# Core bias as two 64-row products, first two relation pairs by node groups, clearing and self bias on GpSimd

## The chip, the cores and the metric

The kernel runs on one core of one Trainium2 chip. The metric is the device time of one execution in microseconds. A measurement is the median of several executions.

## The reference

Two graph layers over 3125 nodes with 256 features, 100,000 edges sorted by destination, 64 edge features and 16 edge types. What is computed, cut to the core:

```
h  = relu(layernorm(x))
ei = concat(h[src], edge_attr)                       # 256 + 64 per edge
core = relu(ei @ W1 + b1) @ W2 + b2
gate = sigmoid(ei @ Wg + bg)
agg  = segment_sum(gate * core, dst)
x    = x + layernorm(agg + h) * gamma + beta
h  = relu(layernorm(x))
forward:  sum over edges into dst of (h @ Wf[type])[src] + forward_bias,  divided by the in-degree
backward: sum over edges into src of (h @ Wb[type])[dst] + backward_bias, divided by the out-degree
x    = x + 2 * h @ loop_weight + self_bias + forward + backward
```

## The kernel before

Nodes lie in 25 blocks of 128, edges in 196 supertiles of 512 (four tiles of 128). Every matrix product of the dense parts is split into three products of rounded high and low parts (PARTS). Each engine runs its own instruction list in order; semaphores tie them together, and there is no planner: the order is written out by hand. It runs in these stages.

*Tables* (to 78 us): layer norm of x, and a table ptab of h @ W1 and h @ Wg for every node, stored in memory.

*Message stage* (to about 1454 us): one pass for each supertile s. GpSimd gathers 4 x 128 rows of ptab into pbuf (two buffers, so the gather for s starts when the first sums of s-2 are done). TensorE runs `edge_products(s)`: twelve 64-row products for the gate into pg (L643), twelve for the hidden layer into pu (L651), both in pairs that lie on the two halves of the array (HALVES: edge features of two tiles are stacked in 64 + 64 partitions), then a wait for the gather and eight transposes of the gathered rows added into pu (L657). Then `core(s-1)`: a wait for s_ulo (low part of the hidden layer), a wait for s_msg (VectorE has read pc), and for each of the two banks of pc a bias product (L666: 128 rows by 512 columns; ones_k times bias_k, of which only the first two partitions are not zero: high and low part of b2) and twelve products with W2 (L671). Then `sum_messages(s-2)`, a one-hot product that sums edges by node (L680), and for supertiles that reach into a further node block a second one. VectorE for each supertile: low part of the edge features (L976), gate sum (L971), low part of the hidden layer (L980), message = gate x core out of pc (L1000), one-hot (L994), addition to acc (L1078), low part of the message (L1006). ScalarE makes the high parts, the relu and the sigmoid.

*Node stage* (to about 1530 us): five groups of five node blocks (GB = 5). VectorE for group g: statistics of acc (L836), scales for the second norm of the group before (`ln_scales`, L844 and L845), centre, residual, low part of the transposed blocks (`evacuate_hT`, L857), statistics of res. ScalarE: `node_group(g)`: square roots, the normalised blocks (L438), high parts of the transposed blocks (L526), and copies of projected blocks to pstage (`evacuate`, L261). TensorE: transposes of five blocks (L602), then `project(0, ...)` for them, six products of 512 columns each block (L775). A projection covers a pair of relations q. Five banks (pslots) and five pstage buffers are used in turn, block b uses b % 5; SyncE stores pstage to proj. `slot b` may be written when the copy before it is done (s_pev) and copied when the store before it has landed (s_pst).

*Forward projections* (to 1775 us): TensorE projects all 25 blocks for q = 1, then q = 2 to 7. ScalarE casts the weights' high part (`weights_high`, L541), VectorE makes the low part (`weights_low`, L1156), then sorts: 12 steps of max and match-replace (L1210, L1213) for each q on the edge keys. Ahead of the sort VectorE clears acc (L1199) and adds the self bias to res (L1200); behind it, it writes the rows for the gathers of proj, which start then, and adds the own products (`own` on TensorE, L620; `add_own`, L861).

*Second layer's sums* (to the end): forward gathers and one-hot sums, with the backward projections between them, then backward gathers and sums.

## Time and profile before

| | us |
|---|---|
| runs before | 3843.88, 3847.81, 3848.78 (median 3847.81) |
| profiled execution | 3849.95 |
| its span, first to last instruction | 3848.1 |

| Engine | busy us | share of the span | instructions |
|---|---|---|---|
| TensorE products | 3288.7 | 85% | 21136 |
| TensorE weight loads | 2831.0 | 74% | 21137 |
| VectorE | 2579.7 | 67% | 3930 |
| GpSimd | 2340.2 | 61% | 2362 |
| ScalarE | 976.2 | 25% | 1654 |

The span in 40 equal slices of 96 us; each digit is the busy share in tenths (9 is 90% or more), PEclk the granted clock of TensorE in tenths of full speed:

```profile
PE   6999999999999996998777778878857778787776
...
DVE  6888888888888887887766673333354444444444
ACT  3555555555555544442000000000010000000000
POOL 1666655666665660002776677777777777777775
PEclk8999999999999998999989899999989999999999
```

Slices 2 to 15 are the message stage, slice 16 holds the node stage, slices 17 to 19 the forward projections. In the profile PE is TensorE, PEld its weight loads, DVE VectorE, ACT ScalarE, POOL GpSimd, SP SyncE; L12 is line 12 of the kernel before. Durations of matrix products are modelled ends and overlap, so what a product costs in a full stream is read from the distance of starts or from the chain of work.

### The profile page before, as it was taken

The numbers are of one execution on the slowest core, as the hardware profiler recorded it, in microseconds if no ns is written. First come the engines' busy times: TensorE is split into PE (matmuls) and PEld (weight loads), VectorE is DVE, ScalarE is ACT, GpSimd is POOL, SyncE is SP. The second block draws the span as 40 slices with busy tenths as digits, with TensorE's granted clock in tenths as the row PEclk, the third lists the DMA queues.
The fourth block names the chain that finished last, engine by engine and source line by source line (L and its number), as shares of the span: only waits on it lengthen the run. The fifth ranks groups of instructions, "written<-read, shape, count | busy, mean of one in ns | idle before, by whom it ended". The sixth has DMA issues, their size and how long they took to land.

```text
span 3848.1 us, 74572 instructions
## 1 busy us (share of the span) xinstructions
PE 3288.7 (85%) x21136; PEld 2831.0 (74%) x21137; DVE 2579.7 (67%) x3930; ACT 976.2 (25%) x1654; POOL 2340.2 (61%) x2362
## 2 busy tenths in 40 slices
PE   6999999999999996998777778878857778787776
PEld 4999999999999995887665566666645666665654
DVE  6888888888888887887766673333354444444444
ACT  3555555555555544442000000000010000000000
POOL 1666655666665660002776677777777777777775
PEclk8999999999999998999989899999989999999999
DMA  5666666666565652664555557555533333333333
GB/s 173 174 171 171 172 171 168 171 168 169 167 169 164 170 160 84 208 209 160 158 163 153 151 154 164 166 157 161 160 97 105 104 102 98 100 105 104 104 105 114
DMA packets 322741, 569.88 MB, mean 148 GB/s; under 512 B 73895, under 2 KB 218389, under 8 KB 322581
## 3 DMA queue, kind: packets, MB, share of 16 engines
q0 software_dynamic: 137984, 411.19, 38.5%
q1 hardware_dynamic: 182732, 154.33, 12.2%
q10 hardware_dynamic: 1864, 2.52, 0.2%
q8 instruction: 65, 1.06, 0.1%
q14 instruction: 96, 0.78, 0.1%
HBM read 452.43 MB, written 115.41 MB: 148 GB/s over the span
## 4 chain that ended last, share of the span: by engine, by line
PE 64%; DVE 15%; issue 10%; POOL 4%; DMA 3%; DVEq 2%; ACT 1%; SPq 1%; ACTq 0%; POOLq 0%
PE pc L671 14%; PE pa L680 13%; PE pa L719 7%; PE pu L657 5%; DVE tops L1210 5%; PE pu L719 4%; PE pg L643 4%; DVE key L1213 4%; PE pg L719 4%; POOL fa L422 4%; PE pu L651 3%; PE pc L666 2%; DMA fa<-proj,gslot 2%; PE pu L775 2%; PE pg L775 1%
## 5 line engine op out<-in xcount | busy, mean ns | idle before, releaser
L422 POOL DMA_INDIRECT fa<-proj,gslot x1568 | 1503.5, 959 | 882.0 <-issue 436.8
L405 POOL DMA_INDIRECT fa<-ptab,slot x784 | 832.9, 1062 | 576.5 <-issue 298.9
L680 PE MATMUL pa<-fa,onehot 128*128 128x258 f32 x1760 | 471.0, 416 | 212.3 <-DVE onehot L994 141.4
L671 PEld LDWEIGHTS pc<-ws,hr 128*128 128x128 f32 x4704 | 607.1, 188 | 16.8
L671 PE MATMUL pc<-ws,hr 128*128 128x256 f32 x4704 | 614.0, 279 | 0.0
L994 DVE SCALAR_TENSOR_TENSOR fa<-pc,base,src_f 128x512 f32<-128x512 f32 x406 | 303.6, 751 | 450.0 <-PE pa L719 320.0
L680 PEld LDWEIGHTS pa<-fa,onehot 128*128 128x128 f32 x1760 | 349.6, 205 | 319.2 <-issue 264.0
L719 PE MATMUL pa<-fa 128*128 128x258 f32 x1568 | 373.5, 380 | 0.0
L719 PEld LDWEIGHTS pa<-fa 128*128 128x128 f32 x1568 | 297.0, 189 | 45.2
L719 PE MATMUL pu<-fa 128*128 128x258 f32 x784 | 198.9, 397 | 120.7 <-DVE acc L1051 82.5
L1000 DVE TENSOR_TENSOR fa<-fa,pc 128x1024 f32<-128x1024 f32 x196 | 239.4, 1221 | 92.4 <-PE pc L671 92.3
L495 ACT CAST hr<-fa 128x1024 fp32r<-128x1024 f32 x196 | 206.4, 1053 | 362.3 <-DVE fa L1000 362.3
L719 PEld LDWEIGHTS pu<-fa 128*128 128x128 f32 x784 | 146.5, 194 | 170.2 <-DVE acc L1051 112.8
L719 PE MATMUL pg<-fa 128*128 128x258 f32 x784 | 194.4, 390 | 85.9 <-issue 85.2
L484 ACT ACTIVATE hr<-pu 128x512 fp32r<-128x512 f32 x392 | 213.3, 596 | 189.1 <-PE pu L657 189.1
L580 ACT COPY gslot<-row_dst 128x8 int32 (+1 forms) x98 | 19.3, 197 | 953.6 <-DMA fa<-proj,gslot 953.6
L1026 DVE TENSOR_TENSOR acc<-acc,pa 128x258 f32 x196 | 82.7, 422 | 261.1 <-PE pa L680 258.7
L1006 DVE TENSOR_TENSOR hr<-fa,hr 128x1024 fp32r<-128x1024 f32 x196 | 240.1, 1225 | 24.8 <-ACT hr L495 9.1
L680 PE MATMUL pa<-hr 128*128 128x256 f32 x1760 | 247.5, 283 | 5.8 <-issue 3.7
L775 PE MATMUL pu<-hr 128*128 128x512 f32 x960 | 251.6, 406 | 0.0
L719 PEld LDWEIGHTS pg<-fa 128*128 128x128 f32 x784 | 145.0, 192 | 132.4 <-issue 112.2
L489 ACT ACTIVATE fa<-fa 128x1024 f32<-128x1024 f32 x196 | 208.1, 1062 | 130.7 <-DVE fa L971 130.7
(151 smaller groups left out, 4934.9 us busy)
## 6 DMA issues: line engine op xcount, KB each, us to landing
proj<-fa SPq DMA_DIRECT2D x400, 256.0 KB, 2.3
fa<-in_ea_t SPq DMA_DIRECT2D x196, 128.0 KB
fa<-proj,gslot POOLq DMA_INDIRECT x1568, 2.8
fa<-ptab,slot POOLq DMA_INDIRECT x784
fa<-in_Wrel SPq DMA_DIRECT2D x32, 256.0 KB, 3.0
ptab<-fa SPq DMA_DIRECT2D x25, 256.0 KB, 2.0
out<-res SPq DMA_DIRECT2D x4, 768.0 KB
res<-in_x SPq DMA_DIRECT2D x1, 1792.0 KB, 20.4
```

What stands on the lines that cost most here:

```text
L405: pool.indirect_dma_start(pbuf[:, n % 2, j, :], None, ptab[:, :], bass.IndirectOffsetOnAxis(ap=slot[:, n, j:j + 1], axis=0)).then_inc(s_ga ...
L422: pool.indirect_dma_start(gbuf[:, n, j, 0:H], None, proj[k - 1][:, :], bass.IndirectOffsetOnAxis(ap=gslot[:, at, j:j + 1], axis=0)).then_i ...
L484: last = nc.scalar.activation(uT[:, par, 0, h, :, :].rearrange("p k e -> p (k e)"), pu[:, h, :], ACT.Relu)
L489: nc.scalar.activation(gate[:, par, :, :], gate[:, par, :, :], ACT.Sigmoid).then_inc(s_gate, 1)
L495: nc.scalar.copy(msg[:, par, 0, :, :], gate[:, par, :, :]).then_inc(s_mhi, 1)
L671: last = nc.tensor.matmul(pc[:, j, :], uT[:, par, a, j // 2, kk, j % 2 * P:(j % 2 + 1) * P], w2s[:, c, kk, :], start=False, stop=(j == jj ...
L680: last = nc.tensor.matmul(pa[:, bank, 0:width], keys[:, at, j, :], rows[:, j, :], start=(n == 0), stop=(n == len(todo) - 1))
L719: last = nc.tensor.matmul(out[:, 0:AW], onehot2[at // GS][:, at % GS, j, :], gbuf[:, n, j, :], start=(j == 0), stop=(j == J - 1))
L775: last = nc.tensor.matmul(pslots[n], hT[:, a, kk, b * P:(b + 1) * P], wsp[:, u, c, kk, :], start=(not d and m == 0 and kk == 0), stop=(m = ...
L994: return nc.vector.scalar_tensor_tensor(out=(onehot0, onehot, onehot2[at // GS])[k][:, at % GS, :, :], in0=nodes, scalar=base[:, bass.ds(b ...
L1000: nc.vector.tensor_tensor(gate[:, par, :, :], gate[:, par, :, :], pc[:, :, :], ALU.mult).then_inc(s_msg, 1)
L1006: nc.vector.tensor_tensor(msg[:, par, 1, :, :], gate[:, par, :, :], msg[:, par, 0, :, :], ALU.subtract).then_inc(s_mlo, 1)
```

## The change

Core bias: `core_bias(s)` writes each bank of pc with one 64-row product of 512 columns; the two banks' products lie on the two halves of the array (partitions 0 to 63 and 64 to 127 of ones_k and bias_k). For that b2 is also brought to partitions 64 and 65 (one more small DMA on ScalarE's queue, four more small VectorE operations). It is issued in edge_products(s) for supertile s-1, between the pu products and the gathered rows' transposes, with the wait for s_msg ahead of it; core() has neither any more. For the first and the last supertile it stands by itself.

First two relation pairs: within each node group TensorE projects the group for q = 0 and then for q = 1, with the next group's transposes in between (three ahead of q = 1's blocks, two among them). The order of the bank uses, of the copies on ScalarE and of the stores follows (slot_use, projected). weights_high(1) moves to ScalarE's first node group, weights_low(1) to VectorE's third loop turn ahead of the scales, weights_low(2) to behind the third step of the first sort.

GpSimd clears acc and adds the self bias, when all blocks are transposed; VectorE waits for that only ahead of add_own.

```diff
+        bias_raw2 = fa[DE:DE + 2, 6144:6144 + H].rearrange("p (d f) -> p d f", d=1)
+        def piped(q):
+            return isinstance(q, int) and q < 2
+        def slot_use(q, b):
+            return 2 * (b // GB) + q if piped(q) else 5 * q + b // 5
+        def projected(q, b):
+            return 2 * GB * (b // GB) + GB * q + b % GB if piped(q) else NB * q + b
         def evacuate(eng, copy, q, b):
-            n = b % 5
-            eng.wait_ge(s_proj, NB * q + b + 1)
-            if b >= 5:
-                eng.wait_ge(s_pst[n], 16 * (5 * q + b // 5))
-            elif past(q, 1):
-                eng.wait_ge(s_pst[n], 16 * 5 * q)
+            n, use = b % 5, slot_use(q, b)
+            eng.wait_ge(s_proj, projected(q, b) + 1)
+            if past(use, 1):
+                eng.wait_ge(s_pst[n], 16 * use)
...
# GpSimd, behind the gathers of the message stage
+            pool.wait_ge(s_hT[1], NB)
+            nc.gpsimd.memset(acc[:, :, :], 0.0).then_inc(s_zero[0], 1)
+            nc.gpsimd.tensor_tensor(res[:, :, :], res[:, :, :], sbias_b[:, :].unsqueeze(1).to_broadcast([P, NB, H]),
+                                    ALU.add).then_inc(s_sb, 1)
# ScalarE
             def weights_high(q, par, half):
-                    act.wait_ge(s_proj, NB * (q - 1))
+                    act.wait_ge(s_proj, 2 * NB - GB if isinstance(q, int) and q == 2 else NB * (q - 1))
                 if g == 0:
                     weights_high(0, 0, 0)
-                for n in range(GB + 1):
-                    if 1 <= g <= NB // GB and n < GB:
+                    weights_high(1, 1, 0)
+                for n in range(GB):
+                    if 1 <= g <= NB // GB:
                         normalise(2, group(g - 1)[n], res, ACT.Relu)
-                    if g >= 2 and n >= 1:
-                        evacuate(act, nc.scalar.copy, 0, group(g - 2)[n - 1])
-                    if 1 <= g <= NB // GB and n >= 1:
-                        transposed_high(group(g - 1)[n - 1])
+                    if g >= 3:
+                        evacuate(act, nc.scalar.copy, 1, group(g - 3)[n])
+                for n in range(GB):
+                    if 2 <= g <= NB // GB + 1:
+                        evacuate(act, nc.scalar.copy, 0, group(g - 2)[n])
+                    if 1 <= g <= NB // GB:
+                        transposed_high(group(g - 1)[n])
...
             weights_high(2, 0, 1)
-            for b in range(NB):
-                evacuate(act, nc.scalar.copy, 1, b)
+            node_group(NB // GB + 2)
# TensorE
+            def core_bias(s):
+                if past(s, 1):
+                    pe.wait_ge(s_msg, s)
+                for h, half in enumerate(HALVES):
+                    nc.tensor.matmul(pc[:, 2 * h:2 * h + 2, :], ones_k[half, :], bias_k[half, 0:1, :].to_broadcast([DE, 2, H]),
+                                     start=True, stop=False)
             def edge_products(s, par, pair):
...
+                if past(s, 2):
+                    core_bias(s - 1)
                 pe.wait_ge(s_gath[0][par], 16 * J * (pair + 1))
             def core(s, par):
                 pe.wait_ge(s_ulo, s + 1)
-                if past(s, 1):
-                    pe.wait_ge(s_msg, s)
                 for jj in range(0, J, 2):
-                    nc.tensor.matmul(pc[:, jj:jj + 2, :], ones_k[:, :], bias_k[:, 0:1, :].to_broadcast([P, 2, H]),
-                                     start=True, stop=False)
...
+            for b in group(0):
+                transposes(1, b)
             for g in range(NB // GB):
-                for b in group(g):
-                    transposes(1, b)
...
                     project(0, 0, b, 0)
-            pe.wait_ge(s_wlo, 2)
-            for b in range(NB):
-                project(1, 1, b, 0)
+                later = group(g + 1) if g + 1 < NB // GB else []
+                for b in later[:3]:
+                    transposes(1, b)
+                if g == 0:
+                    pe.wait_ge(s_wlo, 2)
+                for n, b in enumerate(group(g)):
+                    project(1, 1, b, 0)
+                    for t in later[3 + n:4 + n]:
+                        transposes(1, t)
# VectorE
             split_row(bias_k[0:2, :, :], bias_raw)
+            split_row(bias_k[DE:DE + 2, 0:1, :], bias_raw2, DE)
-                if g == 1:
-                    weights_low(0, 0)
+                if g in (1, 2):
+                    weights_low(g - 1, g - 1)
...
-            weights_low(1, 1)
             dve.wait_ge(s_hT[1], NB)
...
-            nc.vector.memset(acc[:, :, :], 0.0).then_inc(s_zero[0], 1)
-            nc.vector.tensor_tensor(res[:, :, :], res[:, :, :], sbias_b[:, :].unsqueeze(1).to_broadcast([P, NB, H]),
-                                    ALU.add).then_inc(s_sb, 1)
-            dve.wait_ge(s_zero[0], 1)
-            dve.wait_ge(s_sb, 1)
...
                 for n in range(S1):
                     sort_step(before + 2 * n, n)
+                    if also and n == 2:
+                        weights_low(2, 0)
```

## Rows read from the trace of the kernel before

**Rows 1.** Busy time by stretch: busy us (instructions) by engine, clock, DMA, GB/s.
```profile
400.00:1400.00 1000.00, 999.53 (x9610) 948.50 (x9608) 889.61 (x1044) 508.28 (x788) 607.51 (x573) 1.00 0.61 169
1461.00:1540.00 79.00, 52.64 (x219) 40.39 (x220) 63.24 (x200) 37.65 (x87) 0.00 (x0) 0.82 0.27 92
```

**Rows 2.** Chain that ended last, one supertile: start us, us, what.
```profile
1005.91 0.23 PE pc L666
1006.14 1.40 PE pc L671 x12
1007.54 0.23 PE pc L666
1007.77 1.41 PE pc L671 x12
1009.18 0.95 PE pa L680 x8
1010.13 0.90 PE pg L643 x12
1011.03 0.71 PE pu L651 x12
1011.74 1.02 PE pu L657 x8
```

**Rows 3.** Waits, 400 to 1400 us, VectorE: total us, times, longest.
```profile
DVE fa L1000 <- PE pc L671: 68.0, 143, 1.2
```

**Rows 4.** Timeline, a gather's last issue: start us, us, engine, line.
```profile
1005.83 1.01 POOL L405 DMA_INDIRECT fa<-ptab,slot  x1 [0.30 <-issue]
```

**Rows 5.** Chain that ended last, a gather's landing.
```profile
1248.14 3.53 DMA fa<-ptab,slot
```

**Rows 6.** Timeline, start of the message stage, [idle before, releaser].
```profile
80.20 0.55 DVE L900 CAST bias_k<-fa 2x512 fp32r<-2x512 f32 x1
...
82.08 0.74 DVE L903 SCALAR_TENSOR_TENSOR bias_k<-fa,ident,bias_k 2x512 fp32r<-2x512 f32 x1
...
88.22 1.55 PE L643 MATMUL pg<-ws,hr 64*128 64x256 f32 x12 [0.46 <-DVE fa L971]
```

**Rows 7.** Timeline, second node group.
```profile
1479.87 4.06 PE L775 MATMUL pu<-hr 128*128 128x512 f32 x12
...
1481.07 1.72 DVE L836 BATCH_NORM_STATS2 stats<-res 128x6 f32<-128x256 f32 x5
...
1485.48 0.17 DVE L845 SCALAR_TENSOR_TENSOR nmr<-mv,rstd 128x5 f32<-128x5 f32 x1
```

**Rows 8.** Chain that ended last, projections of the node stage.
```profile
1483.93 2.72 PE pg L775 x12
...
1492.13 4.34 PE pu L775 x12
```

**Rows 9.** Groups, ScalarE, 1461 to 1547 us: busy us, mean ns, idle before.
```profile
L438 ACT ACTIVATE acc<-res,nmr,rstd 128x256 f32<-128x256 f32 x25 | 14.7, 606 | 1.6 <-DVE nmr L845 1.6
L261 ACT COPY fa<-pu 128x512 f32<-128x512 f32 x13 | 7.4, 581 | 1.5 <-PE pu L775 1.5
```

**Rows 10.** Timeline, VectorE from the node groups into the sort.
```profile
1530.26 0.42 DVE L857 TENSOR_TENSOR hr<-pa,hr 128x256 fp32r<-128x256 f32 x1 [0.34 <-ACT hr L526]
...
1534.10 5.43 DVE L1199 MEMSET acc<- 128x6450 f32 x1 [1.41 <-issue]
...
1546.30 1.23 DVE L1156 TENSOR_TENSOR hr<-fa,hr 128x1024 fp32r<-128x1024 f32 x1
1547.44 0.97 DVE L1210 MAX8 tops<-key 128x8 f32<-128x784 f32 x1
...
1554.36 0.98 DVE L1210 MAX8 tops<-key 128x8 f32<-128x784 f32 x1
```

**Rows 11.** Timeline, end of the projections and of the sort.
```profile
1774.78 1.58 PEld L620 LDWEIGHTS pa<-ws,hr 128*128 128x128 f32 x12
...
1782.97 0.17 DVE L1219 COPY srt<-tops 128x16 f32<-128x16 f32 x1
```

More of the change, by code:

```diff
@@ L26 @@
 EPS = 1e-5
-NW = 11
+NW = 12
 XA = 10
@@ L345, in _ @@
             sp.dma_start(wlraw.rearrange("p (k f) -> p k f", k=HK), Wl.rearrange("(k p) f -> p k f", p=P)).then_inc(s_w2, 16)
-            with sp.Fori(0, NQ // 4) as i:
+            for q in range(2):
+                sp.wait_ge(s_wlo, q + 1)
+                load_weights(q + 2, q)
+            for g in range(NB // GB):
+                for q in range(2):
+                    store_projections(q, 0, group(g))
+            with sp.Fori(1, NQ // 4) as i:
                 relations(i, 0)
@@ L1247, in sort_region @@
                     keep_sorted(before + 2 * steps, SI // 2 * i + S2 * u, steps)
-            weights_low(2, 0)
-            for q in range(2):
-                sort_relation(q)
+            sort_relation(0, also=True)
+            sort_relation(1)
             with dve.Fori(1, NQ // 4) as i:
```

27 lines of the change are left out of this document (15 added, 12 removed).

## Prediction

> **What bounds the kernel now.** I read four views in this order. First the busy time by stretch [rows 1]: in the message stage (92 to 1454 us) TensorE is busy 999.5 of 1000 us at the full granted clock (1.00, the 2.4 GHz level), while VectorE has 110 us to spare; in the node stage behind it (1461 to 1540) TensorE is busy 52.6 of 79 us and its granted clock is 0.82 on average. So the same TensorE instruction is worth its full time in the first stretch and perhaps nothing in the second. Second, the chain of work that ended last, through one supertile of the message stage [rows 2]: eight TensorE pieces that sum to 6.85 us, nothing else between them. The two bias products are two of them, 0.23 us each. Third, VectorE's waits there [rows 3]: 68.0 us over 143 supertiles are waits for the core products, so 0.475 us of a supertile is what TensorE could give up before VectorE takes over. Fourth, the order of time from the end of the message stage to the second layer's gathers [rows 10, 11]: VectorE closes the node groups at 1530.68, clears sums and adds the self bias until 1546.3, starts sorting at 1547.44 and ends at 1783.1; TensorE has finished projecting before, at 1774.8. There VectorE's chain sets the end.
>
> **The core bias.** Removed are 2 x 196 products of 128 rows by 512 columns at 0.23 us each: 0.46 us a supertile, all on the path [rows 2]. Added are two products of 64 rows by 512 columns, one on each half of the array, behind the other 64-row products of edge_products. The trace of before has no 64-row product of 512 columns. Nearest rows: twelve 64-row products of 256 columns take 0.71 us, or 0.059 each, and twelve 128-row ones of the same width take 1.40, or 0.117 [rows 2]. So two halves run side by side in the time of one, and the pair should cost what one 512-column product costs, 0.23 us. Bounds: 0.12 (the pair as cheap as four 256-column pieces at half of 0.059) and 0.46 (one after the other). I take 0.23, as it follows from both rows. The group L657 already follows a 64-row group today, so no change of mode is added. Saved: 0.23 x 196 = 45 us, bounds 0 and 67.
>
> The wait for s_msg moves with it: the bias of supertile s-1 is issued in edge_products(s), so it waits for messages(s-2) 0.95 + 0.90 + 0.71 = 2.56 us after the core products of s-2 end [rows 2]. Behind it in TensorE's queue stand the gathered rows' transposes, and ScalarE and VectorE wait for those. That message product starts right at the end of the core products and takes 1.22 us, so 1.3 us are left: I cost the wait at nothing. It costs 0.1 us for every 0.1 us by which VectorE is later than that.
>
> What is late next: VectorE needs (1000 - 68) / 143 = 6.52 us a supertile against 1000 / 143 - 0.23 = 6.76 for TensorE, so 0.24 us stay [rows 1, 3]. The gathers are closer. Four are issued in a row; the last began at 1005.83, took 1.01 and needs 3.5 us to land, so 1010.4, and the transposes that read it come at 1011.74 [rows 2, 4, 5]. 1.4 us are left, and a gather has two supertiles, so 0.46 of it goes. Some gather instructions take longer than that one, so a few supertiles will wait. I take 4 us for it, with bounds 0 and 25 (0.13 us in each). Message stage: -45 + 4 = -41 us, likely -20 to -46.
>
> **The start.** The bias is split a second time on VectorE, four small operations in a chain. The first four took from 80.20 to 82.82, 2.6 us, for 512 columns; now 256. Behind them on VectorE stands the first gate sum, for which TensorE already waited 0.46 us, so all of it counts [rows 6]. With the added DMA issue ahead of ScalarE's first work: +2 us, bounds 0 and 3.5.
>
> **The node groups.** Here I have to build the new order. Let N(g) be the moment at which VectorE has the scales of group g's predecessor ready, 1485.65 for g = 2 [rows 7]. Prices: a projected block 1.36 (2.72 for two) [rows 8], its copy by ScalarE 0.58, a normalised block 0.6 [rows 9], two transposes 0.25 (a quarter of L657's 1.02) [rows 2], a low part 0.42 and weights_low 1.2 [rows 10], a high part as much as a low one (an estimate, it reads the same tile) and the cast of weights 1.1 likewise, statistics 2.12 a group and scales 0.35 (1481.07 to 1485.65 holds two and one) [rows 7].
> - weights_low(1) now stands ahead of the scales for g = 2: 1.2 us, N(2) = 1486.9. ScalarE normalises five blocks (to 1489.8) and copies one projected block, TensorE projects two blocks with two transposes between them until 1493.5; high and low part, two statistics and scales give N(3) = 1499.
> - From g = 3 on each normalised block is followed by the copy of relation 1's block of three groups back, and only that copy frees the bank for relation 0's next group. So TensorE waits for N(g) + 1.2, projects five blocks (6.8), transposes three (0.75), then block, transpose, block, transpose (3.2): N + 12.0. Latency and high and low part 1.0, two statistics 4.25, scales 0.35: 17.6 us a group, where today's products of two groups start at 1479.87 and 1492.13, 12.3 apart [rows 7, 8]. TensorE works 15 of these and still idles 2.6. N(4) = 1516.6; N(5) needs one statistic less but waits for a square root: 1532.4.
> - The last low part ends 13.0 later, at 1545.4, where it was 1530.7 [rows 10]: 14.7 us later.
> - Then clearing and adding, 12.2 us from 1534.10 to 1546.30, are gone from VectorE, and so are the two weights_low in front of the sort. Sorting starts at about 1546.5 against 1547.44 [rows 10].
>
> So the move to GpSimd only pays back what the new coupling takes. Then three steps run (6.92 us, to 1553.4) [rows 10], and VectorE waits for the high weights of relation 2, behind which the whole sort is queued. ScalarE has these after TensorE's last block of relation 0: N(5) + 16.1 + 6.8 = 1555.3, copy and cast 1.7, weights_low 1.2: 1558.3, where three steps were done at 1554.36 before. That is +3.9 us, and the sort behind it is unchanged. After sparse transposes TensorE fell to half clock today and took 4.34 us for twelve products that otherwise take 2.72 [rows 1, 8]; three groups can meet that, 0 to +4.8. I take +5 in all, bounds -6 (below) and +12.
>
> GpSimd's part is hidden: it needs to be done when VectorE adds the own products, after 1783, 236 us later [rows 10, 11]. Even at ten times VectorE's 12.2 us it is. If that cover were gone, it would be 12 us or more. TensorE's earlier end of relation 1 is worth nothing: relation 3 needs weights that VectorE makes between sorts, and the gathers wait for the sort's end too. From there on nothing changes.
> The Trainium skill speaks against this move: "GPSIMD Engine Reference", Engine selection, puts a two-input elementwise addition at about twice VectorE's time; by it the addition takes some 14 us (an estimate). It would add that only if it stood on the path; no run here shows it yet.
>
> **Sum.** Profiled execution 3849.95 us (span 3848.1 and 1.9 around it). 3849.95 - 41 + 2 + 5 = 3816. The median of the runs, 3847.81, lies 2.1 below that execution, so I forecast 3814.
>
> **The rivals.**
> - *Another resource takes over in the message stage.* For: gathers have 1.4 us of slack and VectorE 0.24 after the change; the gather queue shows instructions of uneven length. Against: TensorE waited for them almost never over 1000 us. If half of the 45 are lost: 3850 - 22 + 7 - 2 = 3833. Chance 0.15.
> - *The node groups gain.* If VectorE keeps its pace, the second products only fill TensorE's gaps: 45 blocks and their transposes from 1479.8 on, 61.2 + 5 us, end at 1546.0; copy, cast and low part 2.9: 1548.9, 5.5 us earlier than 1554.36. Then 3850 - 41 + 2 - 5.5 - 2 = 3803. Against it: the bank that is freed only behind N(g). Chance 0.15.
> - *The sort is slowed by GpSimd.* Both work in SBUF for 20 us or so; if VectorE's steps took half as long again in that time, 10 us more: 3824. Chance 0.05. "GPSIMD Engine Reference", Specifications, of the Trainium skill, says that the two engines get in each other's way where VectorE's instruction has two SBUF inputs or runs in a two-port mode; the sort's steps have one large input, and by that rule this does not happen.
> - *The two 64-row products do not run side by side* (slower). Both write pc, in two banks, with 512 columns each, a form no row shows. Then the pair costs 0.46, nothing is saved, and start and node groups remain: 3850 + 2 + 5 - 2 = 3855. If each also pays the 0.19 us by which L643 is above L651 for entering its mode, 3892. It decides from a pair of 0.42 us on. Against it: L651 does just this with 256 columns. Chance 0.08.
> - My forecast, 0.57.
>
> **How the numbers follow.** A measurement of this kernel tells about 0.2% from no change, 7.7 us: faster is below 3840, slower above 3855.5. The forecast's own range is 3804 to 3828 (message stage -32 to -46, node groups 0 to +10). The 8 in 10 take in the first two rivals: 3797 to 3838. Faster 0.86; same 0.06 (a gather-bound stage with a bad node stage, part of the fourth rival); slower 0.08.
>
> **What would show it.** In the profile after: a message-stage period of about 6.62 us with the pair at 0.23 in the chain; VectorE's wait for the core products near 0.24 a supertile; waits for ptab gathers in front of the transposes, few; node groups some 17.5 us apart, with the last low part near 1545 and a wait of VectorE for ScalarE's weights near 1554; the sort's end near 1749 (1788 less the 41 of before, plus 2 of the start). The forecast is wrong if the pair costs over 0.3 us, if the bias waits for VectorE, or if the node groups stay at 12 us.

## The result, and the profile after

The changed kernel takes 3816.88 us, the median of four executions (3810.56 to 3823.66); the kernel before, on the same chip, 3846.21 (3843.88 to 3848.78). The ratio is 0.9926, with a 95% interval of 0.9914 to 0.9938: faster by 0.6 to 0.9%. The forecast was 3814, with 3797 to 3838 as the range. The profiled execution took 3810.56 us, its span is 3808.5. One of the five executions of same_half (below) took 6646.73 us at a mean granted clock of 0.53, where its other four have 0.96, and is left out of that kernel's median.

The head of the page of after (busy us, share of the span, instructions of each engine):

```profile
span 3808.5 us, 74360 instructions
...
PE 3248.9 (85%) x21136; PEld 2785.6 (73%) x21137; DVE 2569.9 (67%) x3932; ACT 976.4 (26%) x1654; POOL 2352.2 (62%) x2364
```

The chain of work that ended last, after, one supertile of the message stage (start us, us, what), which answers to [rows 2]:

```profile
1003.46 0.95 PE pa L708 x8
1004.41 0.90 PE pg L673 x12
1005.31 0.71 PE pu L681 x12
1006.02 0.24 PE pc L661 x2
1006.25 1.03 PE pu L689 x8
1007.28 2.81 PE pc L699 x24
1010.09 0.95 PE pa L708 x8
```

The two bias products (L661) are one piece of 0.24 us behind the other 64-row products, where [rows 2] has two pieces of 0.23; the supertile takes 6.63 us instead of 6.85. It is still TensorE from end to end.

The waits of 400 to 1300 us, after (us in total, times, longest), which answer to [rows 3] and to the gathers of [rows 4, 5]:

```profile
DVE fa L1036 <- PE pc L699: 34.4, 76, 0.9
...
PEld pu L689 <- DMA fa<-ptab,slot: 1.5, 4, 0.4
```

The stretch holds 133 supertiles (900 us at 6.78 us each, the 1321.5 us from the first core product to the last by 195; some supertiles carry a further one-hot product, so the mean is above the 6.63 of a plain one). A supertile has 34.4 / 133 = 0.26 us left before VectorE would be late (0.475 in [rows 3]), and TensorE waited for a gather four times, 1.5 us in all.

The node groups of after: VectorE's scales (nmr) from the third on (the first are at 1435.00), and what TensorE waited for (start us, us, idle before and its releaser in brackets), against [rows 7, 8]:

```profile
1459.66 0.16 DVE L881 SCALAR_TENSOR_TENSOR nmr<-mv,rstd 128x5 f32<-128x5 f32 x1
1477.26 0.17 DVE L881 SCALAR_TENSOR_TENSOR nmr<-mv,rstd 128x5 f32<-128x5 f32 x1
1493.29 0.17 DVE L881 SCALAR_TENSOR_TENSOR nmr<-mv,rstd 128x5 f32<-128x5 f32 x1
...
1461.08 2.97 PE L805 MATMUL pu<-hr 128*128 128x512 f32 x12 [2.56 <-ACT fa L272]
...
1478.68 3.00 PE L805 MATMUL pu<-hr 128*128 128x512 f32 x12 [2.56 <-ACT fa L272]
```

From the third to the fourth scales it is 17.60 us, and before each of these groups TensorE idles 2.56 us for ScalarE's copy (fa L272), which stands behind a norm in ScalarE's queue.

Into the sort and out of it, after, against [rows 10, 11]:

```profile
1506.18 0.42 DVE L893 TENSOR_TENSOR hr<-pa,hr 128x256 fp32r<-128x256 f32 x1 [0.86 <-ACT hr L548]
...
1507.10 0.98 DVE L1240 MAX8 tops<-key 128x8 f32<-128x784 f32 x1
...
1518.20 1.23 DVE L1193 TENSOR_TENSOR hr<-fa,hr 128x1024 fp32r<-128x1024 f32 x1 [4.33 <-ACT hr L563]
1519.35 0.97 DVE L1240 MAX8 tops<-key 128x8 f32<-128x784 f32 x1
...
1519.06 14.35 POOL L427 TENSOR_TENSOR res<-res,sbias_b 128x6400 f32<-128x6400 f32 x1 [6.89 <-issue]
...
1742.88 1.58 PEld L643 LDWEIGHTS pa<-ws,hr 128*128 128x128 f32 x12
...
1749.30 0.17 DVE L1249 COPY srt<-tops 128x16 f32<-128x16 f32 x1
```

The sort starts right behind the last low part, stops after three steps for 4.33 us (ScalarE's high weights of relation 2), and goes on beside GpSimd's addition, which takes 14.35 us where VectorE took 6.76. TensorE, which has projected relation 1 early, stops later for the low part of relation 3's weights, which stands in VectorE's queue behind the second sort:

```profile
1568.49 1.22 DVE L1193 TENSOR_TENSOR hr<-fa,hr 128x1024 fp32r<-128x1024 f32 x1
...
1569.85 5.48 PE L805 MATMUL pu<-hr 128*128 128x512 f32 x12 [12.45 <-DVE hr L1193]
```

Where the 39.6 us between the two spans come from: the first core product starts 1.6 us later (94.06 against 92.5); from there to the first statistics of the node stage 1328.7 us pass instead of 1369.4 (-40.7); from there to the sort's end 326.7 instead of 321.2 (+5.5); behind the sort 2059.0 instead of 2065.0 (-5.9). Nothing shows the last to be of the change: in the ten profiled executions on the chips of usual speed, of both biases and both orders of the projections, that stretch took 2059 to 2072 us, and executions of one kernel lie up to 20 us apart.

### The profile page after: what moved, and what is told of

It is laid out like the page before. It is cut to its first block, busy times and chain, and to the rows that moved or that the text cites. A ratio compares the mean times of both kernels' runs of the same rounds, so it can differ in the third digit from the quotient of the medians.

```text
span 3808.5 us, 74360 instructions
## 1 busy us (share of the span) xinstructions
PE 3248.9 (85%) x21136; PEld 2785.6 (73%) x21137; DVE 2569.9 (67%) x3932; ACT 976.4 (26%) x1654; POOL 2352.2 (62%) x2364
## 4 chain that ended last, share of the span: by engine, by line
PE 68%; DVE 13%; issue 10%; POOL 4%; DMA 3%; DVEq 2%; ACT 1%; ACTq 0%; POOLq 0%; SPq 0%
PE pc L699 14%; PE pa L708 13%; PE pa L747 7%; PE pu L689 5%; PE pg L673 4%; PE pu L747 4%; POOL fa L443 4%; PE pu L805 4%; PE pg L747 4%; DVE tops L1240 3%; PE pu L681 3%; PE pg L805 3%; DVE key L1243 3%; DMA fa<-proj,gslot 2%; DVE onehot L1030 1%
## 5 line engine op out<-in xcount | busy, mean ns | idle before, releaser
L699 PE MATMUL pc<-ws,hr 128*128 128x256 f32 x4704 | 598.8, 283 | 0.0
L708 PEld LDWEIGHTS pa<-fa,onehot 128*128 128x128 f32 x1760 | 349.4, 205 | 316.1 <-issue 261.1
L699 PEld LDWEIGHTS pc<-ws,hr 128*128 128x128 f32 x4704 | 565.4, 189 | 0.6 <-issue 0.6
L747 PE MATMUL pu<-fa 128*128 128x258 f32 x784 | 199.3, 397 | 118.2 <-DVE acc L1087 73.4
L805 PE MATMUL pg<-hr 128*128 128x512 f32 x960 | 241.1, 393 | 0.0
```

The costliest lines, as they stand in the source:

```text
L699: last = nc.tensor.matmul(pc[:, j, :], uT[:, par, a, j // 2, kk, j % 2 * P:(j % 2 + 1) * P], w2s[:, c, kk, :], start=False, stop=(j == jj ...
L708: last = nc.tensor.matmul(pa[:, bank, 0:width], keys[:, at, j, :], rows[:, j, :], start=(n == 0), stop=(n == len(todo) - 1))
L747: last = nc.tensor.matmul(out[:, 0:AW], onehot2[at // GS][:, at % GS, j, :], gbuf[:, n, j, :], start=(j == 0), stop=(j == J - 1))
L805: last = nc.tensor.matmul(pslots[n], hT[:, a, kk, b * P:(b + 1) * P], wsp[:, u, c, kk, :], start=(not d and m == 0 and kk == 0), stop=(m = ...
```

## Experiments

Three sets of four kernels. The first and the third ran on chips on which the kernel before took 3846.8 and 3845.8 us. The second set ran on a chip on which every kernel, the one before too, took 4510 to 4583 us; there only the node stage is read, from the traces. Common to all comparisons of that stage is the table below: us from the first scales of the node stage, in the profiled execution. Three kernels stand in it twice (after and after_again; pool_gated and gated_again; early_gated and early_again): the end of the sort repeats to 0.3, 1.5 and 0.2 us, so less than 1.5 us between two kernels says nothing.

| kernel | last scales | sort starts | TensorE's projections end | sort ends |
|---|---|---|---|---|
| before | 46.5 | 73.3 | 300.8 | 309.0 |
| after | 58.3 | 72.1 | 308.1 | 314.5 |
| after_again | 58.3 | 72.1 | 308.5 | 314.8 |
| bias_only | 46.8 | 73.4 | 302.7 | 309.8 |
| nodes_pool_only | 61.3 | 75.1 | 310.0 | 316.6 |
| bias_pool | 47.1 | 83.0 | 313.4 | 319.8 |
| pool_gated | 46.7 | 69.4 | 301.9 | 308.3 |
| gated_again | 47.6 | 70.0 | 303.4 | 309.8 |
| pool_late | 47.0 | 58.9 | 301.5 | 307.8 |
| early_gated | 53.0 | 65.7 | 297.0 | 303.4 |
| early_again | 53.0 | 65.8 | 296.4 | 303.2 |
| no_pool | 59.9 | 87.3 | 318.6 | 325.0 |
| same_half | 58.3 | 72.0 | 308.4 | 314.7 |
| no_bias | 59.9 | 73.7 | 309.8 | 316.1 |

### The change taken apart

bias_only is the kernel before with the new core bias alone:

```diff
+            def core_bias(s):
+                if past(s, 1):
+                    pe.wait_ge(s_msg, s)
+                for h, half in enumerate(HALVES):
+                    nc.tensor.matmul(pc[:, 2 * h:2 * h + 2, :], ones_k[half, :], bias_k[half, 0:1, :].to_broadcast([DE, 2, H]),
+                                     start=True, stop=False)
```

> The core bias alone is changed: pairs of 64-row products, the second split of b2; node groups, clearing and self bias stand as in the kernel before. My theory (message stage 40.7 us shorter between the first core product and the node stage, start 2 us longer, everything behind it as before): 39 us under the kernel before, ratio 0.990. Rival (part of the gain is given back in the second layer whatever the node stage does, since the changed kernel's median lies only 28 us below): about 30 us, ratio 0.992. Rival (the pair costs twice a single product): no gain.

Measured: 3805.77 us, the median of six (3803.50 to 3821.57), against 3846.83; ratio 0.9893, 0.9876 to 0.9910. That is 41 us less by the medians (39 were expected), and 11 less than the whole change; how firm the 11 are is told at after_again.

nodes_pool_only is the change without the new bias: the first two relation pairs projected by node groups, and GpSimd's two steps.

> The node groups with both relation pairs and the move to GpSimd alone; the core bias as before. My theory (a cycle of 17.6 us a group over the copies of relation 1's blocks, then a wait for relation 2's weights): the sort ends 5.5 us later than before, the total is 5 us above the kernel before, ratio 1.0014. Rival (it gains, as it fills TensorE's gaps): the sort ends earlier and the total is 5 us below. Rival (its cost is larger than the stage itself, because the later stages are disturbed): 10 us or more above.

Measured: 3860.22 us, the median of ten; ratio 1.0028, 1.0018 to 1.0038. The other half of the change costs 11 to 13 us, where 5 were expected: the way was right, the size missed. In the table its sort ends 7.6 us later than before's, 2.1 later than in the whole change; the other 3 to 6 us are not seen up to that point. The 2.1 go with the clock: twice the first twelve products of a group ran slowly, at a mean granted clock of 0.66 and 0.63, so partly at the lower of the two levels (1.2 and 2.4 GHz), where the same twelve take 2.97 and 3.00 us in after, at 1.00. TensorE's wait ahead of them is the same in both (2.56 to 2.58 us), so these rows don't say what decides it:

```profile
1500.21 4.38 PE L796 MATMUL pu<-hr 128*128 128x512 f32 x12 [2.58 <-ACT fa L271]
...
1519.22 4.52 PE L796 MATMUL pu<-hr 128*128 128x512 f32 x12 [2.56 <-ACT fa L271]
```

after_again is the changed kernel once more beside these.

> The changed kernel itself, unchanged, beside the other three on one chip. My theory: the sum of the parts, 39 - 5.5 = 33.5 us under the kernel before, ratio 0.9913, within the first measurement's interval (0.9914 to 0.9938) or just beside it. Rival (parts don't add up): 28 us, and then bias_only plus nodes_pool_only differ from it by 5 us.

Measured: 3816.30 us, the median of six (3806.29 to 3819.08); ratio 0.9911, 0.9897 to 0.9925. The sum of the parts, 33.5 us under the kernel before, was expected; it is 30.5. After minus bias_only is 10.5 us by the medians of the same set, of which the sort's end explains 5.0 (314.8 against 309.8). The other half is not firm: bias_only's six executions fall into four of 3803.50 to 3806.74 and two of 3819.08 and 3821.57, and by the means (3810.1 and 3814.9) the difference is 4.8 us. The profiled execution of bias_only was one of the two long ones, and it is behind the sort that it is long (2071.5 us, where after has 2059.0).

bias_pool is bias_only with GpSimd's two steps:

```diff
+            pool.wait_ge(s_hT[1], NB)
+            nc.gpsimd.memset(acc[:, :, :], 0.0).then_inc(s_zero[0], 1)
+            nc.gpsimd.tensor_tensor(res[:, :, :], res[:, :, :], sbias_b[:, :].unsqueeze(1).to_broadcast([P, NB, H]),
+                                    ALU.add).then_inc(s_sb, 1)
...
-            nc.vector.memset(acc[:, :, :], 0.0).then_inc(s_zero[0], 1)
-            nc.vector.tensor_tensor(res[:, :, :], res[:, :, :], sbias_b[:, :].unsqueeze(1).to_broadcast([P, NB, H]),
-                                    ALU.add).then_inc(s_sb, 1)
```

> The core bias and the move of clearing and self bias to GpSimd; the node stage and the order of projections as before. My theory: VectorE starts its sort 13.6 us earlier, but from then on waits for relation weights that follow TensorE's projections (before, only some 2 us lay between them), so the sort ends 2 us earlier than with the core bias alone: 41 us under the kernel before. Rival (VectorE's chain alone decides): 39 + 13.6 = 52 us under it.

Measured: 3814.68 us (3802.42 to 3821.81), ratio 0.9902, 0.9884 to 0.9920. Both the theory and the rival miss the stage: the sort was to end 2 us earlier than in bias_only or more, and ends 10.0 later. VectorE lost 12.2 us of work, and yet the sort starts 9.6 us later, at 83.0. The timeline of bias_pool, VectorE and GpSimd, shows why:

```profile
1492.71 1.22 DVE L1180 TENSOR_TENSOR hr<-fa,hr 128x1024 fp32r<-128x1024 f32 x1 [0.45 <-ACT hr L557]
...
1505.34 14.66 DVE L1180 TENSOR_TENSOR hr<-fa,hr 128x1024 fp32r<-128x1024 f32 x1 [11.08 <-ACT hr L557]
1519.92 0.96 DVE L1228 MAX8 tops<-key 128x8 f32<-128x784 f32 x1
...
1504.81 14.10 POOL L421 TENSOR_TENSOR res<-res,sbias_b 128x6400 f32<-128x6400 f32 x1 [7.01 <-issue]
```

The same instruction takes 1.22 us at 1492.71 and 14.66 at 1505.34, half a microsecond behind the start of GpSimd's addition; it is done 1.09 us after that ends (1518.91). The next relation's low part is late with it, and TensorE waits 8.8 us for that.

### What holds VectorE for 14.66 us

pool_gated is bias_pool with one wait more, which puts the addition behind that low part:

```diff
             nc.gpsimd.memset(acc[:, :, :], 0.0).then_inc(s_zero[0], 1)
+            pool.wait_ge(s_wlo, 3)
             nc.gpsimd.tensor_tensor(res[:, :, :], res[:, :, :], sbias_b[:, :].unsqueeze(1).to_broadcast([P, NB, H]),
```

> The new bias and GpSimd's two steps with the old order of the projections, as in the run bias_pool, and one wait more: GpSimd starts its addition only when VectorE has written the low part of relation 2's weights. In the trace of bias_pool that low part took 14.66 us (1505.34 to 1520.00) beside GpSimd's addition (1504.81 to 1518.91), where it takes 1.23 us elsewhere. My theory: VectorE's operation with two operands in SBUF is held until GpSimd's addition is over. Then it takes 1.2 us here, the sort starts near 1506.6 instead of 1519.9, TensorE's wait of 8.8 us for a later low part goes, and the sort ends near 1743.5 instead of 1756.8: 13 us less than bias_pool in the trace, a time near 3802. Rival: the 14.66 us has another cause (it waited for ScalarE's part); then it stays and so does the time (3814.7). GpSimd's addition itself should then take 14.1 us or less beside the sort.

Measured, timeline of pool_gated:

```profile
1682.10 1.23 DVE L1181 TENSOR_TENSOR hr<-fa,hr 128x1024 fp32r<-128x1024 f32 x1 [9.57 <-ACT hr L558]
1683.24 0.97 DVE L1229 MAX8 tops<-key 128x8 f32<-128x784 f32 x1
...
1683.42 14.13 POOL L422 TENSOR_TENSOR res<-res,sbias_b 128x6400 f32<-128x6400 f32 x1 [7.35 <-DVE hr L1181]
```

The low part takes 1.23 us behind a wait for ScalarE that is nearly as long as before (9.57 and 11.08 us), TensorE no longer waits for a late low part, and the sort ends at 308.3 instead of 319.8: 11.5 us, 13.3 were expected. ScalarE is no cause; GpSimd's addition is. gated_again repeats it on a chip of usual speed: 1.23 us behind a wait of 11.02. On the second chip the whole execution took 4548.09 us (before 4538.57).

gated_again is the same kernel on the third chip, for its time.

> The kernel of pool_gated once more, for its time. Its sort ended 308.3 us behind the first scales of the node stage, 11.5 us earlier than in bias_pool (319.8) and 1.5 earlier than in bias_only (309.8): 3814.7 less 11.5 by the one, 3805.8 less 1.5 by the other, so 3803 to 3804. Rival: the waits behind the sort move with it, and the time stays at 3810 to 3815.

Measured: 3812.96 us, the median of five (3809.42 to 3820.72); ratio 0.9917, 0.9901 to 0.9932. A miss: 3803 to 3804 was expected, and the time is the rival's (3810 to 3815). In its profile the sort ends where it should, 10.1 us ahead of bias_pool's in the table; behind the sort it took 2066.0 us where bias_pool's took 2061.9, and by the medians 1.7 of the 10 us are left. With spreads of 11 and 19 us in the two kernels the medians can't settle the rest.

Against bias_only the gated move gains nothing that can be told: the sort ends at 308.3 and 309.8, bias_only's at 309.8, and the time, 3812.96, is not below bias_only's 3805.77. With the old order of the projections 12.2 us less work on VectorE buy no earlier end. The next run shows why.

pool_late is pool_gated with the low part of relation 2's weights taken from the front of the sort to behind its fifth step.

```diff
+                    if also and n == 4:
+                        weights_low(2, 0)
...
-            weights_low(2, 0)
```

> As pool_gated, and the low part of relation 2's weights is moved behind the fifth step of the first sort, so that VectorE doesn't wait 11 us for ScalarE's part of these weights. The sort starts near 1494.3, 12 us earlier than in pool_gated, and ends near 1732. But TensorE's projections ended at 1738.3 in bias_only and would end near 1741 here, so they take over as the bound: I expect 2 to 3 us less than pool_gated, near 3800. Rival: the sort alone sets the end of the stage; then 12 us less than pool_gated, 3790.

Measured (4538.71 us on the second chip): the sort starts 10.5 us earlier, at 58.9, and ends 0.5 us earlier, at 307.8, which is within the 1.5 us by which pool_gated and gated_again differ (2 to 3 were expected). TensorE's projections end 0.4 earlier, and in them TensorE waits for nothing but a copy, 0.6 us; VectorE now waits 12.1 us in all for ScalarE's high weights, which wait for TensorE. So here TensorE bounds the stage: its projections end at 301.5, and at 300.8 in the kernel before, whatever VectorE is spared. In the other kernels with the old order the sort takes 235.7 to 239.8 us from its start to its end; here it takes 248.9.

### The node groups

early_gated is the changed kernel with ScalarE's copies of relation 1 moved out of the norms: they follow the group's square root. The low part of relation 2's weights goes from behind the third to behind the fifth sort step.

```diff
                     if 1 <= g <= NB // GB:
                         normalise(2, group(g - 1)[n], res, ACT.Relu)
-                    if g >= 3:
-                        evacuate(act, nc.scalar.copy, 1, group(g - 3)[n])
...
                 if g < NB // GB:
                     sqrt_var(2, g, GB * g, GB * (g + 1))
+                elif g > NB // GB:
+                    weights_high(2, 0, 1)
+                for n in range(GB):
+                    if g >= 2:
+                        evacuate(act, nc.scalar.copy, 1, group(g - 2)[n])
...
-                    if also and n == 2:
+                    if also and n == 4:
```

The same blocks are copied, at the end of one group's turn instead of in the middle of the next.

> The changed kernel with ScalarE's copies of relation 1 moved from between the norms of the next group to behind that group's standard deviation, and the low part of relation 2's weights two sort steps later. My theory says that a node group's 17.6 us are ScalarE's: with the copies out of the way, the cycle falls to TensorE's 14.9 us, and the sort ends 10 to 12 us earlier than in the changed kernel's trace, near 1738; time near 3806. If the low part of the weights falls beside GpSimd's addition, which this version doesn't prevent, it takes some 14 us and the sort gives 13 us back: then 3816 or a little above. Rival: the cycle is bound elsewhere and stays at 16 to 17.6 us, time within 3 us of 3816.

Measured on the second chip: 14.96 us from the third to the fourth scales instead of 17.60, 13.36 to the fifth instead of 16.03, the sort's end 11.1 us earlier than in the changed kernel (303.4 against 314.5). The time, 4543.51 us, says nothing beside a kernel before that spread from 4514 to 4558. The low part of relation 2's weights did not fall behind the addition. early_again is the same kernel on the third chip.

> The kernel of early_gated once more, for its time. In its trace the sort of the first layer ended 303.4 us behind the first scales of the node stage, against 314.5 in the changed kernel and 309.8 in bias_only. By that it is 11 us faster than the changed kernel and 6 us faster than bias_only: 3805 and 3800 by their medians, I take 3803. Rival: what is behind the sort (the second layer) gives the gain back: within 3 us of the changed kernel's 3816.

Measured: 3804.06 us, the median of five (3800.88 to 3811.29); ratio 0.9899, 0.9884 to 0.9914; 12.2 us less than after_again by the medians, on another chip. The ratios of the two to their kernels before (0.9899 and 0.9911) have intervals that overlap, so it is the traces that carry this gain. Its trace (scales, then VectorE's low part and GpSimd's addition):

```profile
1459.74 0.17 DVE L882 SCALAR_TENSOR_TENSOR nmr<-mv,rstd 128x5 f32<-128x5 f32 x1
1474.71 0.17 DVE L882 SCALAR_TENSOR_TENSOR nmr<-mv,rstd 128x5 f32<-128x5 f32 x1
1488.07 0.17 DVE L882 SCALAR_TENSOR_TENSOR nmr<-mv,rstd 128x5 f32<-128x5 f32 x1
...
1512.12 1.22 DVE L1194 TENSOR_TENSOR hr<-fa,hr 128x1024 fp32r<-128x1024 f32 x1
...
1513.11 14.22 POOL L427 TENSOR_TENSOR res<-res,sbias_b 128x6400 f32<-128x6400 f32 x1 [7.22 <-issue]
```

This is what the grouping is worth once nothing couples it to the norms: TensorE's projections end at 296.4, 4 us and more ahead of every kernel with the old order, and the sort at 303.2. The copies' new place alone shows in the last scales, 5.3 us earlier (53.0 for 58.3), and in the sort's start, 6.3 earlier. The other 5 us up to the sort's end come behind that: there is no stop of 4.33 us in the sort any more. For that three things changed at once, TensorE's earlier end of relation 0, ScalarE's high weights ahead of the copies, and the low part two steps later; no run takes them apart. It also shows how near the other hazard is: the low part began 0.99 us before the addition. In the trace of after it began 0.86 us before (1518.20 and 1519.06). In both VectorE came first and lost nothing. The small loss is GpSimd's: where the addition began before the low part was over, it took longer by about the overlap (0.42, 0.37, 0.27, 0.23 and 0.08 us of overlap and 14.40, 14.35, 14.25, 14.22 and 14.12 us in nodes_pool_only, after, after_again, early_again and no_bias; 14.10 to 14.14 without any).

no_pool is the changed kernel with clearing and self bias back on VectorE, ahead of the first sort:

```diff
-            nc.gpsimd.memset(acc[:, :, :], 0.0).then_inc(s_zero[0], 1)
-            nc.gpsimd.tensor_tensor(res[:, :, :], res[:, :, :], sbias_b[:, :].unsqueeze(1).to_broadcast([P, NB, H]),
-                                    ALU.add).then_inc(s_sb, 1)
...
+            nc.vector.memset(acc[:, :, :], 0.0).then_inc(s_zero[0], 1)
+            nc.vector.tensor_tensor(res[:, :, :], res[:, :, :], sbias_b[:, :].unsqueeze(1).to_broadcast([P, NB, H]),
+                                    ALU.add).then_inc(s_sb, 1)
```

> The changed kernel with the clearing of the sums and the addition of the self bias back on VectorE, ahead of the first sort. They took 5.43 and 6.76 us there, 12.2 together; VectorE is the engine on which the sort runs, and the sort ended 6.4 us behind TensorE's projections in the changed kernel. My theory: 12 us more than the changed kernel, 3828. Rival: the low part of relation 2's weights and TensorE's own pace hide some of it: 5 to 6 us more, 3822.

Measured (4555.39 us on the second chip): VectorE's two steps take 5.43 and 6.76 us again, the sort starts 15.2 us later than in after (87.3 against 72.1; in after a stop of 4.33 us comes later) and ends 10.5 us later (12 were expected). Of that, 1.6 us were there before VectorE's two steps (last scales at 59.9 instead of 58.3), so the move to GpSimd is worth some 9 us in this order, in the traces. By time it is only seen that no_pool is above the kernel before of its chip (ratio 1.0031, 1.0011 to 1.0052). What the move would be worth with the low part behind the addition, no run in this order shows; in the old order, bias_pool, it cost 10 us.

### The core bias

same_half is the changed kernel with both products on the same 64 rows.

```diff
-                for h, half in enumerate(HALVES):
+                for h, half in enumerate((HALVES[0], HALVES[0])):
```

> The changed kernel with both products of the core bias on the same 64 rows, so that they can't lie side by side; everything else, the 64 rows of each and the result too, is as it was. My theory: the pair costs 0.23 us instead of 0.46 because the two products run at once on different halves of the array. On one half they run one after the other: 0.46 to 0.48 us in the chain of a supertile, a period of 6.86 instead of 6.63 us, and 45 us more over 196 supertiles, 3861 where the changed kernel has 3816. Rival: the gain comes from the smaller product (64 rows instead of 128), or from its place behind the hidden layer; then the pair stays at 0.24 us and the time at 3816.

Measured: 3859.75 us, the median of four (3857.90 to 3863.93); ratio 1.0036, 1.0021 to 1.0051. That is 43.5 us more than after_again, where 45 were expected. The chain of same_half:

```profile
1003.97 0.71 PE pu L681 x11
1004.68 0.46 PE pc L661 x2
1005.14 1.02 PE pu L689 x8
1006.16 2.81 PE pc L699 x24
```

The same two products, of the same shape and in the same place, take 0.46 us on one half and 0.24 on two, and 0.46 is what the two 128-row products took in [rows 2]. So the smaller product and its new place are worth nothing that is seen; the gain is that the two run side by side.

no_bias is the changed kernel without the core bias; b2 is left out of the messages:

```diff
-                for h, half in enumerate(HALVES):
-                    nc.tensor.matmul(pc[:, 2 * h:2 * h + 2, :], ones_k[half, :], bias_k[half, 0:1, :].to_broadcast([DE, 2, H]),
-                                     start=True, stop=False)
```

> The changed kernel with the core bias left out altogether (b2 is not added). What is left of the 0.24 us in a supertile goes from TensorE's chain. If TensorE alone sets the period, it falls from 6.63 to 6.39 us and the time by 47 us to 3769. My theory: VectorE takes over as the bound before that, since its own instructions of a supertile add up to some 6.5 us: a period of 6.5 to 6.55, 16 to 25 us less, near 3795.

Measured: 3802.43 us, the median of four (3790.64 to 3805.57); 14 us less than after, where 16 to 25 less and a time near 3795 were expected: a miss. The core products of the message stage, from the view of one line (count; ns least, median, most; first and last start in us; shapes). Before:

```profile
L671 PE MATMUL pc<-ws,hr x4704: 274/280/288, 92.8 to 1453.9; 128*128 128x256 f32 x196
```

After:

```profile
L699 PE MATMUL pc<-ws,hr x4704: 277/280/415, 94.7 to 1416.2; 128*128 128x256 f32 x196
```

same_half:

```profile
L699 PE MATMUL pc<-ws,hr x4704: 277/280/581, 94.5 to 1455.8; 128*128 128x256 f32 x196
```

no_bias:

```profile
L696 PE MATMUL pc<-ws,hr x4704: 277/280/562, 94.1 to 1386.5; 128*128 128x256 f32 x196
```

From first to last start: 1361.1, 1321.5, 1361.3 and 1292.4 us. The first 0.22 us off the pair gave 39.6 us, 0.20 a supertile. The next 0.24 gave 29.1, or 0.15 a supertile: here something else is reached. (By the medians only 14 of the 29.1 us are seen; the profiled execution, 3790.64, was the shortest of the four, and the others have no trace.) I had named VectorE. The chain of no_bias from 600 to 1300 us, by line, names a loop:

```profile
by line: PE pc L696 27.6%; PE pu L686 10.1%; PE pa L705 10.0%; DMA fa<-ptab,slot 9.1%; issue 7.6%; PE pg L670 6.9%; DVE fa L1033 6.0%; PE pu L678 5.4%; ACT hr L517 5.3%; DVE fa L1004 3.7%; DVE hr L1013 3.1%; DVEq L285 2.5%; DVE hr L1009 0.6
```

A gather's landing holds 9.1% of it (1.0% in after), VectorE's lines some 13%, and VectorE is busy 841.4 of 900 us, not all of them. By this chain the next bound is a loop of gather, transposes, VectorE and the next gather, not VectorE's own rate; no run changes the gathers to prove it. A supertile takes 1292.4 / 195 = 6.63 us on average (6.78 in after), above the 6.52 at which VectorE would be the bound. The expectation went wrong in that, and in setting this mean of 6.52 beside the 6.63 of a plain supertile.

## Why the prediction was right, and where not

**The core bias: right in size and mechanism.** The pair came to 0.24 us for 0.23, the supertile to 6.63 for 6.62, and same_half shows that it is the two halves at work. The stage gave 40.7 us for the 41 worked out, though made up otherwise: 0.22 x 196 = 43, less 1.5 us of waits for gathers in the 900 us looked at, for which I had put 4 for the whole stage, less 1.7 for the last 24 core products, which take 4.55 us in the chain where the others take 2.81 (the granted clock was 0.72 on average from 1411 to 1417), and 0.9 more because the last one-hot products ran slowly in the trace of before (2.08 us at 0.73) and not here (1.22). The clock at the stage's end was in no term of mine; that it nearly cancels is luck. The Trainium skill, "TensorEngine Tiling (Array Packing)", Tiling Modes, has it that different tiles of the array "can execute LdWeights and Matmul in parallel"; 0.24 against 0.46 us is this case's number for it, with 512 columns.

**The wait moved ahead of the transposes, costed at nothing: right.** No wait of L661 is in the chain, nor among the stage's longer waits.

**The start: right.** The second split takes from 82.16 to 83.78, 1.6 us, and TensorE's first wait for the gate sum grows from 0.46 to 2.41:

```profile
82.16 0.28 DVE L936 CAST bias_k<-fa 2x256 fp32r<-2x256 f32 x1
...
89.31 1.65 PE L673 MATMUL pg<-ws,hr 64*128 64x256 f32 x12 [2.41 <-DVE fa L1007]
```

The net is +1.6 us for the +2 forecast.

**The node groups: right, step by step up to the fourth sort step.** The scales were worked out for 1499, 1516.6 and 1532.4, which less the 39.1 us by which the stage begins earlier are 1459.9, 1477.5 and 1493.3; they were done at 1459.82, 1477.43 and 1493.46. The end of the last low part: 1506.3 by the forecast, 1506.60 measured. The fourth sort step: 1519.2 and 1519.35. The sum was +5, the trace says +5.5, and here luck has a part: the +5 were 3.9 of the steps and some 1 for the half clock. The half clock didn't come; instead the rest of the sort, which I had as unchanged, took 1.3 us more, of which 0.5 are waits for ScalarE's later high weights. The coupling named there, a bank that is freed only behind a norm, is what early_again takes away, and the cycle falls from 17.60 to 14.97 us. In after the groups ran at 2.97 and 3.00 us for twelve products; in nodes_pool_only the slow clock did come, for 4.38 and 4.52. That TensorE's earlier end of relation 1 is worth nothing was right too, and for the reason given: TensorE stands 12.45 us at 1569.85 for weights that VectorE makes behind the second sort.

**VectorE's chain sets the end: right, by less than it looked.** I read from [rows 11] that TensorE is done 8 us before the sort. pool_late shows that this is no slack: with the sort starting 10.5 us earlier the stage gains 0.5. In the old order of projections both engines bound this stage within a few us of each other. It did no harm to the sum, since the sort ended where it was put. My rival for the node groups ("5.5 us earlier, 3803") was wrong for this kernel, since the bank is freed only behind the norm; with that taken away, in early_again, the sort ends 5.8 us earlier than before's and the time is 3804.

**GpSimd's part is hidden: right here, and for a reason that the prediction only half had.** The addition took 14.35 us, and 236 us of cover were there. But the cover is not the point. VectorE's low part of the weights reads two tensors in SBUF, and where it starts behind GpSimd's addition it stands still until that ends: 14.66 us in bias_pool, 1.23 in pool_gated. My rival on this looked at the sort's steps alone, found them safe, and they are: they stay 2.31 us apart beside the addition (1519.35, 1521.65, 1523.96). It missed the one VectorE instruction between them that has two such inputs, although it named the rule. Its price, 10 us more, is by coincidence that of bias_pool's sort. In the changed kernel the low part comes 0.86 us first, and no wait sees to that. The Trainium skill, "SBUF — State Buffer", Who interferes with whom, says just this: a VectorE instruction with two SBUF inputs contends with a GpSimd instruction that reads SBUF, the first to start has the port for its whole length, and "Issue order, not op shape, decides who blocks." Both orders are in these traces, and they agree. On the price of the addition the estimate by the Trainium skill, "GPSIMD Engine Reference", Engine selection, was 14 us for 14.35 measured.

**What the prediction said of behind the sort: "nothing changes".** Not testable to better than 13 us a single execution. The profiled execution was forecast at 3816 and took 3810.56: up to the sort's end the trace gives 33.6 us for the 34 forecast, and the 5.9 behind it were in no term. By the medians the kernel before came to 3846.21 with a fourth execution, so the gain is 29.3 us for the 34 forecast (3847.81 less 3814), and the median 3 us above the forecast. Both differences are within the spread of executions.

What the numbers of the forecast don't tell: GpSimd's and the node groups' part of the change does not pay as it stands. nodes_pool_only is slower than the kernel before (ratio 1.0018 to 1.0038), and bias_only is ahead of the whole change in the same set, by 10.5 us in the medians and 4.8 in the means. With the copies moved, early_again, the whole change reaches 3804.06; that and bias_only can't be told apart, both about 41 us below before.

## What to carry to other kernels

Two products with few rows can be laid on the two halves of the array if each half has its own copy of the operands; here that was worth one product's time (0.46 to 0.24 us). Check it by putting both on one half. When work is moved to GpSimd, list every VectorE instruction with two SBUF inputs in the time that it takes, and put a wait between the two engines' instructions rather than trust the order that a trace happens to show. When an order of work is interleaved more finely, look for copies that free a buffer standing in a queue behind something slow: the interleaving then runs at the pace of the queue. Here moving the copies took the cycle of a group from 17.60 to 14.97 us.

## What the runs showed of the hardware

A VectorE instruction with two SBUF operands (a subtraction, 128 x 1024 values) was held for the whole of a GpSimd addition that began 0.53 us before it (14.66 us instead of 1.23), while VectorE's sort steps, with one large input each, kept their pace of 2.31 us to a hundredth beside such an addition (after). Where VectorE's instruction came first it was GpSimd's that took longer, by about the overlap (14.40 us with 0.42 of overlap, 14.10 to 14.14 with none).

GpSimd cleared 128 x 6450 values in 5.50 us, as fast as VectorE (5.43), and needed 14.1 to 14.4 us for the addition that takes VectorE 6.76.

On one chip all kernels were 18% slower. In the trace of pool_gated there, a core product has its usual median length (280 ns), but the chain has stops: 16% of the span goes to nothing that the profile shows ("issue") and 15% to "another core or an unknown queue", where gated_again, the same kernel on the third chip, has 10% and none. The mean granted clock is 0.89 instead of 0.96. The message stage ends some 178 us later; the node stage takes what it takes elsewhere (the sort ends at 308.3 and 309.8); the rest is behind the sort. The chain of pool_gated in the message stage:

```profile
999.99 1.17 PE pc L693 x10
1001.16 0.55 issue
1001.72 1.81 PE pc L693 x14
1003.52 0.95 PE pa L702 x8
```

What holds the engines there isn't known. There the ratios of pool_gated, pool_late, early_gated and no_pool to the kernel before, which carry the new bias too, are 1.0015, 0.9994, 0.9992 and 1.0031: on such a chip nothing of the 41 us is left to see.
